# Three decoder layers of attention on one core: emptying PSUM on other engines and in another order

## What is computed

```
layer 0: x = norm(x + selfattn(x, causal))            with key mask
layer 1: y = norm(x + crossattn(x, ctx))              with key mask
         x = norm(y + relu(y @ w1 + b1) @ w2 + b2)    128 -> 512 -> 128
layer 2: x = norm(x + crossattn(rope(x Wq), rope(ctx Wk), ctx Wv) Wo)
```

## Time and profile before

| | |
|---|---|
| three runs, us | 554.28, 554.58, 556.31 (median 554.58) |
| profiled execution, us | 554.87 |
| its span, first to last instruction, us | 553.0 |
| mean granted TensorE clock | 0.996 of full speed |
| DMA | 12.74 MB, nearly all in the first 24 us; the later weights in four loads of 512 KB |
| chain that ended last | PE 77%, DVE 9%, ACT 6%, POOL 3%, issue 3% |

### The profile page before, as it was taken

The page is one execution under the profiler, slowest core; times in us unless marked ns, Lnnn a source line. Parts: engine busy times, 40 slices in busy tenths (PEclk is TensorE's granted clock), DMA queues, the critical chain, the costliest instruction groups (busy, mean ns, idle before and its releaser), DMA issues.

```text
span 553.0 us, 23802 instructions
## 1 busy us (share of the span) xinstructions
PE 516.1 (93%) x10364; PEld 473.4 (86%) x10364; DVE 419.6 (76%) x784; ACT 370.4 (67%) x1003; POOL 290.5 (53%) x563
## 2 busy tenths in 40 slices
PE   7899999999999899999999999888999999999885
PEld 6789898998988789898888988878888899999775
DVE  4777888767787577777777777887778888888843
ACT  6565766757767657645657575667676787887852
POOL 2214535454354354342624336868676787787724
PEclk9999999999999999999999999899999999999999
DMA  8900000000010110000000000000000000000000
GB/s 243 316 31 3 3 2 2 2 4 2 9 73 1 41 42 1 2 2 4 2 2 3 2 1 3 2 4 1 4 8 9 12 9 9 12 8 9 8 12 15
DMA packets 10838, 12.74 MB, mean 23 GB/s; under 512 B 752, under 2 KB 8432, under 8 KB 10736
## 3 DMA queue, kind: packets, MB, share of 16 engines
q1 hardware_dynamic: 10736, 11.24, 6.7%
HBM read 10.18 MB, written 1.05 MB: 20 GB/s over the span
## 4 chain that ended last, share of the span: by engine, by line
PE 77%; DVE 9%; ACT 6%; POOL 3%; issue 3%; DMA 1%; SPq 0%; POOLq 0%; ACTq 0%; DVEq 0%
PE ps_p L598 14%; PE ps_p L439 10%; PE ps_p L440 8%; PE ps_p L441 8%; PE ps_p L570 6%; PE ps_a L493 5%; PE ps_a L514 5%; PE ps_p L559 4%; PE ps_p L561 3%; PE ps_p L560 3%; PE ps_a L475 3%; PE ps_p L623 3%; PE ps_p L514 3%; DVE turn L825 2%; POOL kT L1046 2%
## 5 line engine op out<-in xcount | busy, mean ns | idle before, releaser
L1064 POOL TENSOR_TENSOR small<-mv,epsilon 128x1 f32<-128x1 f32 x48 | 18.1, 377 | 172.2 <-DVE mv L864 172.2
L598 PE MATMUL ps_p<-wo,headsT 128*128 128x128 f32 x768 | 93.6, 275 | 1.9 <-ACT headsT L670 1.3
L598 PEld LDWEIGHTS ps_p<-wo,headsT 128*128 128x128 f32 x768 | 90.5, 192 | 3.4 <-ACT headsT L670 1.4
L825 DVE TENSOR_TENSOR turn<-ps_p,rope 128x1024 f32<-128x1024 f32 x64 | 76.1, 1221 | 8.1 <-PE ps_p L441 5.6
L698 ACT ACTIVATE headsT<-ps_a 128x512 f32<-128x512 f32 x60 | 32.6, 596 | 69.0 <-PE ps_a L514 69.0
L921 DVE TENSOR_REDUCE total<-probs 128x16 f32<-128x1024 f32 x48 | 58.1, 1211 | 26.5 <-ACT probs L724 19.6
L680 ACT ACTIVATE probsT<-ps_p 128x512 f32<-128x512 f32 x96 | 52.9, 611 | 25.4 <-PE ps_p L570 25.3
L439 PE MATMUL ps_p<-xT_hi,wq_hi 128*128 128x256 f32 x192 | 60.0, 313 | 5.6 <-DVE xT_lo L812 2.9
L714 ACT ACTIVATE probs<-ps_a,top 128x64 f32<-128x64 f32 x256 | 55.9, 350 | 9.7 <-DVE top L893 7.3
L678 ACT ACTIVATE vv<-ps_p 128x512 f32<-128x512 f32 x96 | 57.2, 614 | 1.4 <-PE ps_p L561 1.0
L686 ACT ACTIVATE qT<-ps_p,columns 128x256 f32<-128x256 f32 x96 | 39.0, 489 | 27.3 <-PE ps_p L441 27.3
(11 more groups left out here) (138 smaller groups left out, 1392.8 us busy)
## 6 DMA issues: line engine op xcount, KB each, us to landing
out<-y_out SPq DMA_DIRECT2D x16, 64.0 KB, 1.6
X<-in_x SPq DMA_DIRECT2D x1, 768.0 KB, 8.3
across<-in_across SPq DMA_DIRECT2D x1, 704.0 KB, 10.0
wq_raw<-in_L_xattn_sa_wq SPq DMA_DIRECT2D x2, 256.0 KB, 3.7
wk_raw<-in_L_xattn_sa_wk SPq DMA_DIRECT2D x1, 512.0 KB, 5.6
wv_raw<-in_L_xattn_sa_wv SPq DMA_DIRECT2D x1, 512.0 KB, 7.6
wo<-in_L_xattn_sa_wo SPq DMA_DIRECT2D x1, 512.0 KB, 8.7
wo<-in_L_xattn_ca_wo SPq DMA_DIRECT2D x1, 512.0 KB, 9.6
```

Of the source, the lines that this page charges most:

```text
L598: last = mm(bank[:, 0:E], headsT[:, p, :, :].rearrange("r b q -> r (b q)"), wo[:, layer % 2, p, :], start=(p == 0), stop=(p == PAIRS - 1))
L825: ins = V.tensor_tensor(turn[:, j % 2, :, :].rearrange("d a (h b t) -> d a h b t", h=2, t=S), bank[:, None, :].broadcast_to([128, 2, 512]) ...
```

## The change

ScalarE's list in steps that are not `by_head` becomes: deferred probabilities, O, FT, T of even steps and V first, then both exponentials, then the copies of the weighted heads, then Q or K (`scalar_order`). Transposed probabilities are emptied by VectorE (DD) up to step 29, by ScalarE (AA) in by_head steps and step 46, by both (DA) in steps 47 and 48. Of Q and K VectorE takes bank 3 instead of bank 1. F1's second half goes to ScalarE. Values of steps 16 and 32 are no longer last. In a feed-forward step FT comes first, and both halves of F1 before K.

VectorE's list: the input's low part ahead of the shifts, P after them; in by_head steps sum ahead of Y; the feed-forward statistics (`fstat`) and gain (`fgain`) are steps of their own, the statistics last, the gain a step later from chunk 29 on; `ffn_out` in the second step after its chunk. `inv` and `rinv` get two buffers. Step 45's second half is normalised by VectorE. Splits of new weights move to steps 13, 14, 15 and 29, 29, 31. GpSimd adds up Kr3 in two halves, and scores wait for the half that they read. In steps from 31 on with a feed-forward chunk ScalarE normalises the unit before after F1. The last step's O1 is emptied by VectorE.

```diff
+def turned_by(u):
+    return "AA" if by_head(u) or u == N - 2 else "DA" if u > N - 2 else "DD"
+def rest_by_scalar(u):
+    return by_head(u) and by_head(u + 1)
+def gain_step(f):
+    return f + 1 if f >= 2 * UNITS - 3 else f
 def fills(u):
-    heads = [("O", b, "A") for b in range(2)] if heads_in_ring(u) else []
+    heads = [("O", b, "D" if u == END - 1 and b else "A") for b in range(2)] if heads_in_ring(u) else []
-    probabilities = [("P", j, "A") for j in range(2)] if turns(u) and not defers(u) else []
+    probabilities = [("P", j, turned_by(u)[j]) for j in range(2)] if turns(u) and not defers(u) else []
-            project.append((name + "r", j, "D") if rotary(u) else (name, j, "ADAA"[j]))
-    late = u > 0 and u % UNITS == 0
-    early, late = ([], values) if late else (values, [])
+            project.append((name + "r", j, "D") if rotary(u) else (name, j, "AAAD"[j]))
...
-        return deferred + into + project[:2] + heads + project[2:] + values + inside + result + probabilities + outof + next_in
+        return deferred + into + project[:2] + heads + project[2:] + values + inside + result + outof + probabilities + next_in
     if ffn_chunk(u) is not None:
-        k = len(project) // 2
-        return heads + early[:1] + [("FT", 0, "AD")] + early[1:] + probabilities + project[:2] + [("F1", 0, "A")] \
-            + project[2:k] + [("F1", 1, "D")] + project[k:] + [("F2", 0, "D")] + result + late + next_in
+        return [("FT", 0, "AD")] + values + probabilities + [("F1", 0, "A"), ("F1", 1, "A")] + project + [("F2", 0, "D")] \
+            + result + next_in
     if u % 2:
-        return heads + early + probabilities + project + result
-    k = len(project) // 2
-    return deferred + heads + turn_in + early + probabilities + project[:k] + result + project[k:] + late
+        return heads + values + probabilities + project + result
+    return deferred + heads + turn_in + values + probabilities + project[:3] + result + project[3:]
...
+def rotations(name, j):
+    return (0, 1) if (name, j) == ("Kr", 3) else (1,)
...
     if by_head(u):
...
+        return maxima + those("FT") + those("Qr", "Kr") + before + fgain + [("sum", 0)] + more_weights + fout + those("Y") + ffn \
+            + those("T") + stat
+    head = maxima + before + those("FT") + ([] if u % 2 else those("T")) + [("shift", 0), ("shift", 1)] + those("P")
+    if by_head(u + 1):
+        return head + [("sum", 0), ("norm", 0, u)] + weights + those("K") + [("norm", 1, u)] + fout + more_weights + ffn \
+            + those("Y", "T") + stat
+    if u % 2:
+        return head + more_weights + [("sum", 0), ("norm", 0, u)] + those("K") + [("norm", 1, u)] + weights + fout + ffn \
+            + stat + fgain + those("Y")
+    return head + [("sum", 0), ("norm", 0, u), ("norm", 1, u)] + weights + those("Y", "Q")
...
+def scalar_order(u):
+    emptied = [(at, n, j) for at, (n, j, who) in enumerate(fills(u)) if "A" in who]
+    ahead = [e for e in emptied if e[1] in ("PP", "O", "FT") or e[1] == "T" and u % 2 == 0
+             or e[1] == "V" and (e[2] == 0 or u != N - 1)]
+    return ahead, [e for e in emptied if e not in ahead]
...
+            return {(UNITS - 3, False): (1, 0), (UNITS - 2, False): (1, 1), (UNITS - 1, True): (1, 2),
+                    (2 * UNITS - 3, False): (2, 0), (2 * UNITS - 3, True): (2, 1), (2 * UNITS - 1, True): (2, 2)}\
+                .get((u, after_input))
...
-                if layer == 2 and v == 0:
-                    pe.wait_ge(rotated, ROTATED.before(u))
+                if layer == 2:
+                    pe.wait_ge(rotated, ROTATED.at(u - 1 - v, "Kr", 3, v))
...
+                        if (name, j) == (("F1", 1) if ffn_chunk(u) is not None else ("V", 1)):
+                            split_high(u, after_input=True)
+                            if by_head(u - 1):
+                                normalise_rest(u - 1)
...
+                ahead, behind = scalar_order(u)
+                for at, name, j in ahead:
                     empty(u, at, name, j)
...
+                if attends(u):
+                    for j in range(2):
+                        exponentials(u, j)
+                if finishes(u) and not heads_in_ring(u):
+                    heads_out(u)
...
+                for at, name, j in behind:
+                    empty(u, at, name, j)
...
+                elif name == "P":
+                    ins = V.tensor_copy(probsT[:, j, :], bank[:, :])
```

More of the change, by code:

```diff
@@ L186, in vector_order @@
         return (emptied[:1] + [("weights", 0), ("weights", 1)] + emptied[1:]) if u < 0 else emptied
-    before = [("norm", u - 1, 0)] if by_head(u - 1) else []
-    ffn_out = [("fout", 0)] if ffn_chunk(u - 1) is not None else []
-    if by_head(u):
-        n = 4 if ffn_chunk(u) is None else 5
-        turn_in = [e for e in emptied if fills(u)[e[1]][0] == "T"]
-        early, late = ([("weights", 0)], []) if u == 2 * UNITS else ([], [("weights", 0)])
-        return [("max", 0)] + ([] if split_heads(u) else [("max", 1)]) + emptied[:n - 2] + early + emptied[n - 2:n] + before \
-            + [e for e in emptied[n:] if e not in turn_in] + ffn_out + [("sum", 0)] + late + turn_in
@@ L197, in vector_order @@
-    head = [("max", 0)] + ([] if split_heads(u) else [("max", 1)]) + before + [("shift", 0), ("shift", 1)]
-    n = 1 if u % 2 == 0 and projected(u) is not None or ffn_chunk(u) is not None else 0
-    return head + emptied[:n] + [("sum", 0)] + emptied[n:n + 1] + [("weights", 0), ("norm", u, 0)] + emptied[n + 1:n + 2] \
-        + [("norm", u, 1)] + emptied[n + 2:] + ffn_out
+    before = [("norm", j, u - 1) for j in range(1 if rest_by_scalar(u - 1) else 2)] if by_head(u - 1) else []
+    maxima = [("max", 0)] + ([] if split_heads(u) else [("max", 1)])
@@ new lines, in vector_order, with those @@
+    fgain = [("fgain", 0)] if gained(u) is not None else []
+    fout = [("fout", 0)] if ffn_chunk(u - 2) is not None else []
+    names = [fills(u)[at][0] for _, at in emptied]
+    def those(*wanted):
+        return [e for e, n in zip(emptied, names) if n in wanted]
+    weights, more_weights = [("weights", 0)], [("weights", 1)]
+    ffn = those("F2")
+    stat = [("fstat", 0)] if ffn else []
+    if by_head(u):
+        return maxima + those("FT") + those("Qr", "Kr") + before + fgain + [("sum", 0)] + more_weights + fout + those("Y") + ffn \
+            + those("T") + stat
@@ L985, in beside_exponentials @@
                     keys_at_all(kind, units, MASKED, count)
+                elif u == 8:
+                    for i in range(4):
+                        of = slice(32 * i, 32 * i + 32)
+                        V.tensor_copy(fold[of, :].rearrange("r (two c) -> r two c", two=2),
+                                      eye_bf[of, None, of].broadcast_to([32, 2, 32])).then_inc(setup_dve, 1)
             def before_m1():
@@ L998, in _ @@
                     keys_at_all(0, slice(0, READY), FIRST_MASKED, FIRST_VALID)
[L999 to L1004 removed]
+                for name, j, *unit in vector_order(u):
                     if name == "max":
```

185 lines of the change are left out of this document (94 added, 91 removed).

## The result

Four runs of the changed kernel took 535.00, 531.65, 534.26 and 533.45 us: median 533.86, against 554.62 for four runs of the kernel before beside them. The ratio is 0.9606 (95% interval 0.958 to 0.9631). The profiled execution took 535.0 us with a span of 533.2, so the span fell by 19.8 where the sum had 23.1.

What follows compares the result with a forecast made beforehand. TensorE, working 516.1 of 553.0 us, was taken as the bound, so only its standing could be won. Gains less losses of seven parts summed to 23.1: 554.87 - 23.1 = 531.8, forecast 532.0, range 525.5 to 545.

Steps and rivals of the forecast that it cites:

- part 1: Steps 2 to 29: ScalarE takes inputs and values first, ending projection stops; gains 2.3, 0.2 and 0.6 us.
- part 3: Steps 16 and 17, layer 1's beginning: values in their usual place, stop for instructions counted half; 2.2 us gained.
- part 4: Feed-forward chunk: F1's second half to ScalarE, FT first; 4.0 us in steps 21 to 27, 1.8 at step 29.
- part 7: Last four steps: VectorE normalises step 45's half, P shared, O1 to VectorE; 3.0 of 32.42 us gained.
- part 2: VectorE copies probabilities at 0.62 us each: 1.0 lost in steps 4 to 7, 0.9 in 14 and 15, 0.8 gained (fold).
- part 5: Entry to layer 2: earlier wk_lo, sum and input's low part, F2 waiting less; gains 1.6, 3.4, 1.9 and 1.2 us.
- part 6: Layer 2, even steps 38 to 46: Kr3 rotated in halves lets scores start earlier; 0.4 each, 2.0 us gained.
- A: Rival: no slack, head copies end 0.4 later in steps 2 to 29, 11 us given back: 543 us; chance 0.19.
- C: Rival: VectorE bounds steps 0 to 29, even steps' scores wait for K3, copies of 1.2 us decide: 560; chance 0.03.
- B: Rival: stops only move, GpSimd rotations keep layer 2 as it is, head copies late too: 551 to 553; chance 0.06.
- D: Rival: no instruction stops, no loss in steps 4 to 15, layer 2's entry nearly dense: 525 us; chance 0.06.

Runs made afterwards that it cites:

- best version: Changed kernel plus key flags in even steps, 128 records in front, input's low part behind the shifts from step 14: 526.71 us, 0.9477 of the kernel before.

## Why the prediction was right, point by point

The forecast of 532.0 is 1.9 under the median of 533.86, and the mechanism was the forecast's, not a rival's. But its closeness is in part luck. Parts 1, 3 and 4 gave 4.6 us more than forecast, the rest 7.9 less, and of the 3.3 that this leaves about 1.5 is a fall of the clock that belongs to the profiled execution (part 7); that execution is 1.1 over the median. By the terms of its sum, span against span:

| term | forecast | measured |
|---|---|---|
| part 1: steps 2 to 13; 19; even steps 18 to 28 | 2.3; 0.2; 0.6 | 4.3; 0.3; 1.1 |
| part 2: key flags; steps 14, 15; fold | -1.0; -0.9; 0.8 | -3.7; -0.9; 0.7 |
| part 3: steps 16, 17 | 2.2 | 3.3 |
| part 4: four feed-forward steps; step 29 | 4.0; 1.8 | 4.6; 2.1 |
| part 5: 30/31; 32/33; 34/35; 36/37 | 1.6; 3.4; 1.9; 1.2 | 1.5; 3.3; 1.6; 0.6 |
| part 6: steps 38 to 45 | 2.0 (with 46) | 1.2 |
| part 7: from 46 to the end | 3.0 | 0.3 |
| before step 2 | none | -0.5 |
| sum | 23.1 | 19.8 |

**Part 1, too small: the price of a stop.** I took 0.19 for a stop. Odd plain steps fell by 0.31 (9.64 to 9.33), even ones by 0.40 (9.90 to 9.50). In step 11 before, the starts of the projection's matmuls lie 0.12 apart, but at the stop 127.32, 127.63 and 127.85: 0.31 and 0.22. The first is 0.19 too long, which is what I had counted; the second, behind the stop, is another 0.10. So a stop of 0.19 cost 0.29. In an even step the first Q matmul came 0.1 earlier as well. The order of ScalarE's list and the slack of 0.1 before Y held as worked out; with the heads first most plain steps cost nothing more, and those where VectorE has more to do 0.3 to 0.6.

**Part 2, the failing step: the loss under the key flags.** The copy was sized right (0.62 taken, 0.615 measured), and so was the loss in steps 14 and 15. What failed was "I count 1.0 lost" in steps 4 to 7. Against 9.33 the steps 3, 5 and 7 are longer by 0.64, 1.28 and 1.81: 3.7. I set VectorE's sum of 18.8 us against a pair of 19.2 and priced only the gaps and the fuller steps 6 and 7. But the pair has one deadline, K3 in the odd step, and work in the odd step can't use the even step's spare time. Spreading and then moving the parts to even steps shows it: 3.0 of the 3.7 come back, though the same work is done; the 0.64 of step 3, where masks are prepared, stays. The exchange of K1 and K3 shows that having bank 3 is not the cause.

That the copy costs VectorE more than ScalarE, the rule of the Trainium skill, "Perfetto Trace Analysis", section "Optimizing Scalar/DVE Operations", that I had weighed, agrees with the trace in its sign: 683 ns for the new copies against 611 for ScalarE's, 0.07 apart. But from the start of one copy to the start of the next, which is what a copy costs in a row, it is about 0.60 us on VectorE and 0.48 on ScalarE (medians of 29 and 48 pairs), 0.12 apart. My 0.03 compared a duration with a duration and hid this. It was covered, except in the steps above. The part can't be left out, though: with probabilities on ScalarE the new order loses 28.8 us by step 46.

**Part 3.** The other term was right: 1.7 gained without the stop for instructions, 1.4 forecast. The stop didn't recur, where I had counted half.

**Parts 4 and 5** came out near the sum: 6.7 for 5.8, and 7.0 for 8.1. That a stop's price is more than its idle time bears on part 4 too; that this is the surplus was not tried. In part 5 the 1.5 of steps 30 and 31 has the size forecast (1.6) by luck. In the kernel before, the clock fell to 0.50 behind the wait for `wk_lo`: fifteen projection matmuls started 0.21 apart instead of 0.12, 1.4 us in all, to which I gave nothing. The changed kernel keeps 1.00 there, but its weight loads wait in step 31 for banks that VectorE empties into `turn` (0.60, 0.97 and 0.47 us). First two matmuls of the kernel before in the slow stretch, then the longest of the new stops:

```profile
350.55 0.41 PE L440 MATMUL ps_p<-cT_lo,wk_hi 128*128 128x256 f32 x1
350.76 0.41 PE L441 MATMUL ps_p<-cT_hi,wk_lo 128*128 128x256 f32 x1
```

```profile
341.57 0.39 PE L486 MATMUL ps_p<-x2T_hi,w_hi 128*128 128x256 f32 x1 [0.53 <-DVE turn L887]
```

The pair of steps 32 and 33 is 24.91 where I took 24.8, between bounds of 22.4 and 28.19. Its reason was only half right: "the sum comes ahead of Y" is worth about 1 us, paid for in part by steps 33, 35 and 37, where the turns follow the sum. That is also where 0.6 of step 37 went: it became 0.34 longer, 0.56 shorter again with the sum behind.

**Part 6** held in size, 0.42 a step for 0.4, shown by the experiment. The stop falls at the end of the odd step as I cut them. A new step 44 of 10.55 instead of 10.02 takes 0.5 away; it has a distance of 0.60 between two projection matmuls with nothing awaited, and is back at 10.03 with the records shifted by 128: a stop for instructions as well.

**Part 7, the largest miss.** Of 3.0 only 0.3 came. Step 46 gained 1.04 for 1.5. I put this down to ScalarE's eight normalising instructions; with them back, only 0.35 is lost, and the early sum, which I had not counted here, may hold the rest. From step 47 on 1.5 was forecast and 0.75 was lost. "A second stop for instructions there is left as it is" was true of the stop (1.75 before, 1.65 after), not of what came with it: the granted clock fell to 0.50 and 0.68 behind it, and 47 to 49 took 23.04. Without stop and fall the same steps take 19.71, 3.33 less. The stop's own distance from record to record is 1.87, so about 1.5 is the clock's. The run with the whole rotation agrees: the same stop of 1.87, a clock of 1.00 behind it, and 21.58 from step 47 on, 1.46 less. Without the fall part 7 would have brought some 1.8 of its 3.0. The kernel before, 22.30 with a stop of 1.96 by the same measure and a clock of 1.00, would have some 20.3 without it: so the edits of steps 47 to 49 are worth about 0.6, less than half of their 1.5. This is an estimate from these two traces.

**The rivals.** A and C named the waits to look for. C's, K3 in even steps' scores, is there, in five steps and not in every pair, with copies of 0.62 and not 1.2. A's, head copies late, is there only as the 0.2 in seven even steps that the forecast had. B happened in a small way: TensorE's weight loads wait 4.9 us for banks emptied into `turn`, 1.9 in the kernel before, and 2.0 of the 3.0 that are new lie in step 31. The best version meets two of D's conditions, no long stop for instructions and nothing lost in steps 4 to 7: 526.71 where D had 525.

## What to carry to other kernels

Compare an engine's work with its next deadline, not with the period: VectorE, busy for 93 to 94% of a pair, cost nothing or 1.3 to 1.8 us by which of the two steps the work stood in. Price a short stop by the distances of the starts at it and behind it; here 0.19 cost 0.29 in an odd step. When an engine's list is reordered, ask which other engine must take something over for the order to pay: half of this change alone made the kernel slower. And look at the granted clock on both sides before a stage's gain is put down to an edit: one short fall was worth about 1.5 us here, as much as a whole part of this change.

## What had not been expected of the hardware

**Stops for instructions sit at fixed numbers.** Number all of TensorE's records, semaphore instructions included, by their starts, from 0 on. Then every place between steps 10 and 49, in all fourteen profiles, where two starts lie over 0.7 us apart with nothing awaited is at a number that leaves 193 when divided by 256:

| number | = 256 x | kernel and step | distance of starts, us |
|---|---|---|---|
| 6593 | 25 | before, step 17 | 1.75 |
| 12737 | 49 | K1 for VectorE, flags in seven parts: step 32 | 1.35, 0.80 |
| 19137 | 74 | K1 for VectorE, whole rotation, low part late: step 44 | 1.07, 0.86, 1.08 |
| 20673 | 80 | before, after, and nine of the experiments, step 47 | 1.31 to 1.96 |
| 20929 | 81 | 256 records in front, step 47 | 1.59 |

The Trainium skill, "Runtime: NRT & Kernel Launch", section "Instruction fetch mechanics", says that instructions are fetched in blocks of 256 and that this is hidden because they are issued more slowly. The distance agrees; the second half doesn't hold here, where such a place costs up to 1.96. Most of the five lie in the small matmuls of scores or weighted values, where records come fastest; number 19137 lies in a projection behind scores. Shorter ones sit at such numbers too: 0.42 and 0.51 us in steps 32 and 34 of the kernel before, 0.60 in step 44 of the changed one. In both kernels with 128 records in front no place over 0.7 was left, but there are 0.37 in step 16 of both, which is 0.3 to 0.4 longer for it, and 0.43 in step 32 of the best version. Other shifts weren't tried, and that the fast records make the stop is argued, not shown.

**The clock fell behind such a stop, sometimes.** After the stop at 513.97 the granted clock was 0.50, the level of 1.2 GHz, for 2 us and 0.68, a mean over both levels, for the next 2. The same stop in the kernel before left it at 1.00, and so did the ten experiments that have it: one fall in twelve profiles. A fall of the same kind came behind the wait of 1.69 for `wk_lo` in the kernel before. What decides this stays open. The changed kernel's four runs had mean clocks of 0.991, 0.995, 0.997 and 1.0 and took 535.0, 534.26, 533.45 and 531.65 us, in this order.

**Small matmuls in one quadrant** were dear: 6.23 us for the group above. In four quadrants in turn half as many took 1.16 us, and the scores behind them started at 14.65, no later than without them. The first group also wrote to one place of PSUM all the time and the second to four, so which of the two made the difference isn't shown.
